# Four-layer gated cross-attention megakernel: an eight-headed layer's value products in 64-column tiles, row sums taken with the exponential, and a new order of steps

## What is computed

```python
x = x + tanh(g_xattn[0]) * diff_attention(LN(x), ctx)        # layer 0: 32 score heads of 8, values of 16
x = x + tanh(g_ffn[0])   * coupling_net(LN(x))
x = x + tanh(g_xattn[1]) * perceiver(ctx, LN(x), mask)       # layer 1: 8 heads of 64
x = x + tanh(g_ffn[1])   * moe_10_experts(LN(x))
x = x + tanh(g_xattn[2]) * attention(LN(x), ctx, ctx)        # layer 2: 16 heads of 16
x = x + tanh(g_ffn[2])   * attention_then_moe_8(LN(x))       # "f2": 16 heads of 8, then 8 experts
x = x + tanh(g_xattn[3]) * attention_one_head(LN(x), ctx, ctx)
x = x + tanh(g_ffn[3])   * quantised_mlp(LN(x))

# layer 1's attention, the one that the change edits
kv = concat([LN(ctx), LN(x)], axis=tokens) @ Wkv             # 512 keys
sim = (q * 64**-0.5) @ k.T * 64**-0.5                        # masked over the first 256 keys
out = softmax(sim) @ v                                       # 256 queries x 64, for each of 8 heads
out = layernorm(concat(heads) @ Wo)
```

## Time and profile before

| | |
|---|---|
| Time, median of 3 runs | 4502.43 us |
| Lowest, highest | 4487.78, 4503.43 us |
| Profiled execution | span 4493.2 us from first to last instruction; the profile gives no other time of this execution |
| TensorE | busy 4197.2 us (93%) |
| Weight loads | 3198.6 us (71%) |
| VectorE | 2949.1 us (66%) |
| ScalarE | 2085.8 us (46%) |
| GpSimd | 91.9 us (2%) |
| Chain that ended last | PE 80%, DVE 12%, ACT 5% |
| Granted TensorE clock, mean | 0.972 |

### The profile page before, as it was taken

One profiled execution on the slowest core, in us unless ns is written; L12 is line 12 of the kernel. 1 busy time (PEld: TensorE's weight loads), 2 busy tenths in 40 slices (PEclk: granted clock), 3 DMA queues, 4 the chain that ended last, 5 costly groups with the idle time before them and its releaser, 6 DMA issues.

```text
span 4493.2 us, 73928 instructions
## 1 busy us (share of the span) xinstructions
PE 4197.2 (93%) x28256; PEld 3198.6 (71%) x28256; DVE 2949.1 (66%) x7812; ACT 2085.8 (46%) x3424; POOL 91.9 (2%) x180
## 2 busy tenths in 40 slices
PE   7898998989989899898999999999999999999998
PEld 4675966759667596675966759667696676956768
DVE  6667776676656666666765767657676576665655
ACT  4544455353553435535355353553535535356342
POOL 0000000000000000000000000000000000000000
PEclk8999999999999999999999999999999999999999
DMA  2010610103001030010300103001030010300012
GB/s 99 1 45 10 217 37 1 52 23 132 29 15 41 24 128 29 15 41 29 123 29 15 41 29 123 29 15 41 29 123 29 15 41 29 123 29 15 31 55 102
DMA packets 51769, 228.06 MB, mean 51 GB/s; under 512 B 4832, under 2 KB 21216, under 8 KB 31584
## 3 DMA queue, kind: packets, MB, share of 16 engines
q1 hardware_dynamic: 51424, 223.33, 13.8%
HBM read 202.34 MB, written 20.97 MB: 50 GB/s over the span
## 4 chain that ended last, share of the span: by engine, by line
PE 80%; DVE 12%; ACT 5%; issue 3%; DMA 0%; SPq 0%; DVEq 0%; ACTq 0%
PE w L574 18%; PE w L584 12%; PE o L709 11%; PE w L830 8%; PE w L820 8%; PE w L642 4%; PE w L558 4%; PE o L702 3%; DVE mx L1243 3%; PE w L625 3%; PE w L677 2%; PE w L567 2%; PE w L721 1%; DVE nt L1184 1%; PE w L612 1%
## 5 line engine op out<-in xcount | busy, mean ns | idle before, releaser
L1243 DVE TENSOR_REDUCE mx<-w 128x4 f32<-128x1024 f32 x512 | 606.8, 1221 | 180.5 <-PE w L625 167.2
L975 ACT ACTIVATE pt_spread<-w 128x1024 f32<-128x1024 f32 x512 | 519.9, 1024 | 236.8 <-PE w L642 203.7
L709 PE MATMUL o<-pt_spread,va 128*32 128x256 f32 x4096 | 543.2, 396 | 30.5 <-ACT pt_spread L975 29.8
L921 ACT ACTIVATE oth<-w,res 128x256 f32<-128x256 f32 x656 | 276.9, 471 | 569.4 <-PE w L820 470.3
L574 PE MATMUL w<-xnT,stream 128*128 128x256 f32 x1792 | 413.1, 382 | 1.4 <-ACT xnT L913 0.8
L574 PEld LDWEIGHTS w<-xnT,stream 128*128 128x128 f32 x1792 | 338.2, 191 | 50.7 <-DVE x L1212 1.0
L709 PEld LDWEIGHTS o<-pt_spread,va 128*32 128x32 f32 x4096 | 205.0, 111 | 202.2 <-issue 63.3
L820 PE MATMUL w<-qodd,va_hi 128*128 128x256 f32 x2048 | 344.8, 283 | 1.1 <-issue 0.8
L820 PEld LDWEIGHTS w<-qodd,va_hi 128*128 128x128 f32 x2048 | 284.6, 188 | 7.8 <-issue 2.4
L1502 DVE TENSOR_REDUCE mx<-w 128x2 f32<-128x1024 f32 x128 | 155.8, 1225 | 199.2 <-PE w L679 198.9
L1212 DVE SCALAR_TENSOR_TENSOR x<-w,gate,x 128x256 f32<-128x256 f32 x512 | 223.2, 477 | 90.6 <-PE w L830 71.7
(11 more groups left out here) (263 smaller groups left out, 7722.5 us busy)
## 6 DMA issues: line engine op xcount, KB each, us to landing
stream_lo<-split SPq DMA_DIRECT2D x56, 1024.0 KB, 4.8
va_hi<-split SPq DMA_DIRECT2D x56, 1024.0 KB, 6.9
stream<-in_moe_dram SPq DMA_DIRECT2D x80, 384.0 KB, 3.1
stream<-in_resident_dram SPq DMA_DIRECT2D x8, 2048.0 KB, 7.4
raw<-in_moe_dram SPq DMA_DIRECT2D x8, 1024.0 KB, 6.8
split<-va_hi SPq DMA_DIRECT2D x8, 1024.0 KB, 8.9
split<-stream_lo SPq DMA_DIRECT2D x8, 1024.0 KB, 10.8
stream<-in_resident_dram SPq DMA_DIRECT2D x8, 1024.0 KB, 4.7
```

The source lines that it names most:

```text
L709: mm = pe.matmul(o[g:g + 32, 0:T], by_heads(plan, s)[:, kt, plan.v_of(h), :], p[:, a * 512 + kt * T:a * 512 + (kt + 1) * T], start=(kt == ...
L921: h = act.activation(dst[:, c, :], w[:, c * T:(c + 1) * T], func, bias=bias[:, c:c + 1], **more)
L975: act.activation(exp_buffer(plan.name + ".exp", s, u), w[:, :], ACT.Exp, scale=scale).then_inc(S["s_P"], 1)
L1243: dve.tensor_reduce(mx[s][:, :, 2 * v:2 * v + 2].rearrange("p t a -> p a t"), w[:, :].rearrange("p (a t k) -> p a t k", a=2, t=TT), AX_X, ...
```

## The change

The eight-headed layer's value products go two heads at a time into one bank: head `u` into partitions 0 to 63 or 64 to 127 by its parity, with 64 columns and a `tile_position`. The ones and their column of `va` are gone; the row sums are taken by the exponential's accumulated output. So an item is two heads, there are 4 evacuations and one `back` step of eight transposes of 128x128 for each element, and the scaling works on the layout of two heads. `ORDER` is laid out anew from end to end.

```diff
-        self.units_per_item = 4 // self.per_unit if group else 1
+        self.units_per_item = 2
...
 ORDER = (
-    "DAM11ADM11ADDAAMAAAA7AAAJAMAAAAAAAMA1AMMAMAD0M050M50M505M0M50M50M50M5M0550M50M50M5M0M505M0M55CC5HC0HCHCHCHCHC2H0CH0CHHC0"
+    "DAM11ADM11ADDAAMAAAA7AAAJAMAAAAAAAMA1AMAADM0M0M50M50M50M50M50M50M50M5M0550M50M50M50M550M0MM55CC5HCHCHCHCH0CHC0HHCC20H0HH"
...
-            va.append(sb(f"va{s}", [P, KT * L1_HEADS * (L1_DIM + 1)]))
-            va_hi.append(nc.alloc_sbuf_tensor_at(f"va_hi{s}", [P, MOE2_COLS], F32R, offset=nc.sbuf_base - KT * L1_HEADS * (L1_DIM + 1) * 4))
+            va.append(sb(f"va{s}", [P, KT * L1_HEADS * L1_DIM]))
+            va_hi.append(over(f"va_hi{s}", [P, MOE2_COLS]))
...
                 if plan is L1:
+                    g = L1_DIM * (u % 2)
                     for kt in range(KT):
-                        mm = pe.matmul(o[0:L1_DIM + 1, 0:T], by_heads1(s)[:, kt, u, :], p[:, kt * T:(kt + 1) * T],
-                                       start=(kt == 0), stop=(kt == KT - 1))
+                        mm = pe.matmul(o[g:g + L1_DIM, 0:T], by_heads1(s)[:, kt, u, :], p[:, kt * T:(kt + 1) * T],
+                                       start=(kt == 0), stop=(kt == KT - 1), tile_position=(0, g))
...
-                m = L1_DIM + 1 if plan is L1 else P
                 for i in range(4):
                     for tt in range(TT):
-                        mm = pe.transpose(w[:, i * T + tt * P:i * T + tt * P + m],
-                                          oth[s][0:m, i, tt * P:(tt + 1) * P], ident[0:m, 0:m])
+                        mm = pe.transpose(w[:, i * T + tt * P:i * T + (tt + 1) * P], oth[s][:, i, tt * P:(tt + 1) * P], ident)
...
-                evac(oth[s][0:m, i % 4, :], bank[0:m, 0:T], "s_oT")
+                evac(oth[s][:, i % 4, :], bank[:, 0:T], "s_oT")
...
                         h = act.activation(turned[s][u % 2][:, tt, :], w[:, tt * 512:(tt + 1) * 512], ACT.Exp,
-                                           bias=mx[s][:, tt, u:u + 1], scale=-1.0)
+                                           bias=mx[s][:, tt, u:u + 1], scale=-1.0,
+                                           accum_out=mx[s][:, tt, L1_HEADS + u:L1_HEADS + u + 1])
...
                 if plan is L1:
-                    v = w[:, :].rearrange("p (i t d) -> p i t d", i=4, t=TT)
-                    r = rc[:, 0:8].rearrange("p (i t) -> p i t", i=4)
-                    link(dve.reciprocal(r, v[:, :, :, L1_DIM]))
-                    o = ob[s][:, :].rearrange("p (t n i d) -> p t n i d", t=TT, n=2, i=4)
+                    dve.wait_ge(*after("s_soft", "l1.soft", s, L1.units - 1))
+                    r = rc[:, 0:TT * L1_HEADS].rearrange("p (t h) -> p t h", t=TT)
+                    link(dve.reciprocal(r, mx[s][:, :, L1_HEADS:2 * L1_HEADS]))
+                    v = w[:, :].rearrange("p (i t h d) -> p i t h d", i=4, t=TT, h=2)
+                    o = ob[s][:, :].rearrange("p (t i h d) -> p t i h d", t=TT, i=4, h=2)
+                    r = r.rearrange("p t (i h) -> p t i h", h=2)
                     for tt in range(TT):
-                        h = dve.tensor_tensor(o[:, tt, k], v[:, :, tt, 0:L1_DIM],
-                                              r[:, :, tt].unsqueeze(2).to_broadcast([P, 4, L1_DIM]), ALU.mult)
+                        h = dve.tensor_tensor(o[:, tt], v[:, :, tt], r[:, tt].unsqueeze(3).to_broadcast([P, 4, 2, L1_DIM]), ALU.mult)
...
                 if st == "l1":
-                    link(pool.memset(qodd[s][0:64, :, :].bitcast(F32), 0.0))
-                    ones = by_heads1(s)[:, :, :, L1_DIM:]
-                elif st == "l3":
+                    pool.memset(qodd[s][0:64, :, :].bitcast(F32), 0.0).then_inc(S["s_vinit"], 1)
+                    return
+                if st == "l3":
```

More of the change, by code:

```diff
@@ new lines @@
+    "HCCNCNCHHCNCC5CHC0NN0CHHC7C3C0HHH30C300C309009C089809C86968C6CCC8L6CK6LKCLKILCL0IIK0I99K8I089069C086L988C6C660LCKLJ0IKKI"
+    "I0L0CKLK0II0CFF0F00F000CC000C0C000C5050ACC50C50CC550C0CC557C5C0C0C0CHCHH00C0C0000HH00C00CH0C00HH0H0C00C000A55JCCC0CCCCC0"
+    "CC50CC50CC550CCC0C55C5C0CC0HCHCHC0HC0BHHCCH0HH0C7CCGC0C04JGBC9CC4L1860K9BI8C60LK9BCIL806K9DMICDB186L09KBCL8I09K6CL8I6B11"
+    "KA0AI9ACALAMA8BAK6I0C9L86DK0IDMC0A0JD0AA0C0AA0MC0M71AAC0CA0AAAAA0AAM0C0MC05050C50M50M50M5C0M50M5MMC5050MM50M50M50M50M5MM"
@@ new lines @@
+    "0CMMCCC55HHCC5H0CHCHCHCHCHCH0HHCC00HCHCHCH0C620HH60H6C020602C0CC000C0C0I0CI0ICI0C0ECE07020C0ECC0CCC0C0JC0CBC0E0BCB0C005B"
+    "0C0B50C050B505CB00CCCB0N0C550NCNC5HCCNCCH5CNHCH0CNCN0CCHHCNC0733CHH0H30C009C3009089C0896896F6C8CCCC6LL8CKKIJ6CLCLKKILK00"
+    "98I90II680968609C988CL660CLCK0KL0IKLII0CLKK0I0ICFF00F0C000000CC0C00A0C5050CC50C50CC550C0CCC555C70C0CCHCHCA000HH00000C00C"
+    "00HHC0C00HHJ0H0C00C00C055CC0C0CCCC55CC0CC05C0C5C0CCCC5545C740CC0HHCC00HC0HCHCHC01HHM0H1CGJC1C1CCA09CGCC8L6KIACLA09KAAI86"
@@ new lines @@
+    "AACL0K98AI6C0L9K8IAD6ACL09KI8A06C9L8AK6IAA09CL86AAKA0I9MD8C6D0710LAA0KAIJ00DD0CM00CMCMAC0MACC0C0CMM00C0M50M50M50M50M50M5"
+    "0M50M50M550M50M50M5M0MCMCM5500CCC55HHCC5HCHCH0C2HCHCHC0HHHC7C0HHCCH0CH0C60HH6E0H602C0602C0CC0E00C0C00ICI0ICI0C0C0200C0EC"
+    "C0CCC0C0C0JCBC0CB0CB005C0B00B5500E0CB055C0B0CCCB00NC550NCCN5HCCNCCH5CNCHH0CNN0CCCH7HN0CC33CHH3H30C00C00F9900C8980C968896"
+    "CCCC6LCKL6ILKCICLKL0KI08CK96II80990L8K89660CI69L88C660LKCCLKJ0ILK0IKII00C0F0F00CC000F000C00A0C05M0C5050C50C50CC5C0CC55CC"
@@ new lines @@
+    "5C0C0C7CMHCHC00HH000000C00C00HHC0C00HH0H0C00C000C55C0ACJC0CCCC55CC0C0C5C0C5C0CCC5C5745C40CC0HH0CC10H0CHCHCHC0HH0H1CGCC1J"
+    "1CCA0C9GCC8LAK60I9CADL86AAKAI09C8LA6AKAI0C9L86KD0I9C8L6AKIACL09KI86DAA09C8L6AAKI0D9AA86C0M0LAA0K7AI0010MCJM0CD0CMM0CCM00"
+    "AAC00C0M50M5M0505050CM50M50M50M5C5500CM55M0M0M50M50MMCMMCCC552HHCC57HCHCHC0HCHCHCH0HHCC02HHCCH0CH0C0HH660H0C60602C0C0C00"
+    "JC00C0ICI0ICI0EC0C0CE0C2C0C0CC0EC0C0C0CB0E0CBBC5000CB00B50050CB550CB00CCCB00N55C0NCNC5HCCNCNCHHCNCC5CHHC0NNC007CCHC3HHH3"
@@ L275 @@
+    "E0CJ002C0ECC0CCC0C0C0CBC0CB0CB5000ECC0B505CB00CCC0NCB550CB00NHC50BCN50HC0NCCN5HCCNCC5H0CN7N0CH0HCC3CHHH30C300C039F0908C8"
+    "09690C68968CCC6CLCLKCLKLICKI0C8IL6090KKL89C9IKI88I60L9068C6968L6CK0CK0LKLII0JKII000CFF0C00F000C000C0C000C5050C5C0C50CC55"
+    "0C0CC5C55C0C0CCHC0HC0H0H0C70000CH00C00H0C0HH0H0J0C00C0005C5C0CC0CCCC55CC0CC05C0C5C0CCC5C545C0CC00HCHCHCHCHCHC0HHH0CC0JCC"
+    "C00C79CC8LK0IC69L8K609ICL8K6ICL09K86IGCL09K8CI60LK98I09C68LK6I0C98L6K0IC400GC00C0C00CCCC00C0CC0C"
 )
```

64 lines of the change are left out of this document (22 added, 42 removed).

## The result

| | before | after |
|---|---|---|
| Time, median | 4497.83 us (4 runs, 4487.78 to 4503.43) | 4544.53 us (4 runs, 4540.51 to 4549.76) |
| After / before | | 1.0104, 95% interval 1.0086 to 1.0123 |
| Profiled execution: time, span | 4493.22, 4493.2 us | 4549.76, 4547.6 us |
| Granted TensorE clock, mean | 0.972 | 0.959 |

The change makes the kernel slower by 1.04%. The forecast was 4398 us, faster by 2.3%.

A forecast was written before the change was run, and what follows sets the result against it. TensorE was taken as the bound, busy 4197.2 of 4493.2 us. The eight-headed layer's 54 us (66 - 15 + 3) and the order's 50 sum to 104, taken from 4502.4 to give 4398 us; range 4335 to 4480.

The forecast's parts named there:

- A pair saves at most the 1.73 us of its second head, less the time by which that head's probabilities come late: Eight-headed layer's value products: 52 pairs of adjacent heads overlap in two column tiles, gaining 66 us after lateness.
- the last tile stands behind twelve others: Argument for 64-column overlap: 16 instructions of 32-column units in four tiles took only 1.03 us.
- The first rival: Eight-headed layer: 64-column tiles do not overlap, since the first head's instructions queue ahead; 4453 us, chance 0.08.
- Changes of tile shape: Eight-headed layer's value products: 76 runs entered and left, 152 changes at 0.10 us, 15 us lost.
- The accumulated output at 0.10: Eight-headed layer's exponentials on ScalarE: 256 row-sum outputs at 0.10 us each, bounds nothing and 0.20.
- So it costs nothing as long as TensorE has more to do than ScalarE: Eight-headed layer: row sums cost nothing, as two heads take TensorE 6.3 us and ScalarE at most 5.7.
- The 94 overlaps of 32 columns: New overlaps in layer 0, layer 2 and its expert layer's attention: 0.79 us each, 61 counted half, 50 us gained.
- Nothing else in the order do I put at a gain or a loss: Whole new order: apart from the overlaps and their changes of tile shape, its effect was put at zero.
- TensorE never stands: Layer 0's value products: TensorE has no idle time, so 33 new overlaps count in full, 26 us.
- signs of being wrong: 16 instructions in 3.4 us; L703's ScalarE waits over 30 us; layer 2 no shorter, more idle TensorE; exponentials much over 0.8 us.
- The one for slower: TensorE stands at the 167 paired runs, behind two score steps lacking a bank; at 1.0 us each 4565 us, chance 0.07.
- The freed time turns into waiting: TensorE waits for ScalarE and VectorE, swallowing two thirds or more; 10 to 35 us stay, about 4480, chance 0.09.

The follow-up runs named there:

- E3: Changed kernel with the products of two adjacent heads of different parity issued in turn: 4509.74 us, ratio 1.0047 to the kernel before.
- E4: Changed kernel without the exponential's accumulated output, row sums left out of the computation: 4528.11 us, ratio 1.0093 to the kernel before.
- E7: Kernel before, with the new order in layer 0's value products alone: 4481.78 us against 4501.41, ratio 0.9960.
- E1: Changed code with the old order, less its first `back` steps and one pair of steps exchanged: 4543.65 us against 4485.76, ratio 1.0120.
- E2: Code of the kernel before with the new order, a few steps of the eight-headed layer adapted: 4627.32 us, ratio 1.0313 to the kernel before.
- E5: Changed kernel with the old order in the experts' stretch alone: 4547.25 us, ratio 1.0115 to the kernel before.
- E9: E3 with the new order only in layer 0 and the eight-headed layer, old order from there to the experts' end: 4529.92 us, ratio 1.0095.
- E10: Kernel before, with the new order only from the eight-headed layer's last value products to the experts' end: 4574.88 us, ratio 1.0183.

## Why the prediction was wrong

**"A pair saves at most the 1.73 us of its second head, less the time by which that head's probabilities come late": wrong.** The second head costs 0.92 us (2.79 less 1.87) at the least, since its instructions can't pass the first head's. 52 pairs save at most 0.81 each, 42 us, where the forecast had 66. The lateness itself was no worse than thought: with the products in turn (E3), which start only when both heads are there, 46 of the 52 pairs take 1.88, and the waits ahead of them are 13.8 us, 0.27 a pair; 0.25 was taken for 41 of them and 1.2 for the other 11. The step that failed is the inference from "the last tile stands behind twelve others": those were four to a tile. The first rival named the danger ("have to be queued before the second head's first") and I argued it away. Its extreme, 0.22 us saved a pair, did not come either; by the Trainium skill's strict order of starts (TensorE: Matmul & The Clock Gate, Part 3, "The mechanism") no second head could start before the eighth instruction of the first, and the trace has it at the fifth.

**Changes of tile shape, 0.10 each: nearly right.** 0.09 at entry and at exit, and 0.05 more inside a run (its first step is 0.27, not 0.22): 0.24 for a single head against 0.20.

**The accumulated output at 0.10: half of what it is** (0.20). "So it costs nothing as long as TensorE has more to do than ScalarE" was close: 4 to 5 us by E4. But the comparison of 6.3 against 5.7 us per pair was one of sums, and a sum does not say when: in a pair's `exp`, `max`, `exp` the next softmax is due before ScalarE can have it.

**The 94 overlaps of 32 columns: right as work.** L710 lost 69.3 us with 123 us more at the low clock in the whole kernel; 50 were counted, 74 before halving. Layer 0 gave 20 of 26 us, in E7 18.

**"Nothing else in the order do I put at a gain or a loss": wrong, and this is what turned the sign.** Standing grew by 91.3 us: 27 in the eight-headed layer, 22 in the attentions, 14 in the experts, 13 in layer 0, where "TensorE never stands" was said of the order of before. The low clock, of which the sum has no term, grew by 123 us, at 0.35 some 43. The page had it beforehand: 0.93 in layer 2's stretch against 1.00 elsewhere. The account: +91 standing, +43 clock, and, as what remains, the rest of TensorE's work down by 80, where the forecast had 104: together +54. Of the signs of being wrong, layer 2's came: the attentions took 745.6 us against 746.8, with 22 us more standing.

**The rivals.** The one for slower was right in that standing ate the gain, but not on where: it put it at the pairs, behind two score steps for want of a bank. L710's and L703's own waits for ScalarE came to 25.5 us (29.8 at L709 before), and the wait for banks (L625 for VectorE) grew by 9.1. The rest stands at transposes, `exp` scores and other steps whose input is late, the transposes' wait by L1124 with 26.0 us more first of all. In size, the rival asked for 0.62 us of standing at each of 167 paired runs; there were 91 / 167 = 0.55, and with the clock 0.80. I gave it 0.07, on the ground that the kernel before meets few such waits, but a row of before speaks for the order of before. "The freed time turns into waiting" had a ceiling at no change that nothing in it justified: moving steps can make more waiting than the work that it saves. E1 and E2 show that code and order have to be priced together, since the same order costs 140 us with the old code.

What stays open: which steps of the new order cost the experts some 32 us, whether the changed use of the banks makes E1's later stretches longer, and why 11 of the 52 pairs start their second head at 1.18 us. No kernel tried here keeps the new order's overlaps in layer 2 without its standing, so that what they would be worth there is reckoned, not measured.

## What to carry to other kernels

When products into different column tiles are to run side by side, issue them in turn, or in blocks of at most four instructions (two fp32 products) a tile; eight in a row into one tile give away about half of the overlap. When a step is moved to sit beside its like, price the standing of all that now follow each other without it, and the low clock that comes with standing, not only the work that overlaps. And of a new order, take over the part by which its stretch gets shorter, where the two orders agree at its ends: layer 0's alone made this kernel faster than either, while the cuts of E5, E9 and E10 lost 27 to 36 us each on the way to the next pass, against the kernel before.

## What the runs showed of the hardware that was not expected

A column tile holds one running and three waiting instructions, and the next instruction for it blocks those for other tiles behind it (2.79, 2.33 and 1.90 us for blocks of 8, 6 and 4). Products into another tile start ahead of earlier ones in the program. An accumulated ScalarE output is a second instruction of 0.20 us. A us at the low clock costs 0.35 us in these stretches, and 0.41 over executions of one kernel, not the 0.5 of a halved speed; that waits cover the rest was not tested. Executions of one kernel differ by 20 us together with the granted clock (4483.6 us at 0.974, 4504.0 at 0.969). And eight needless transposes ahead of each of three waits an element raise the mean clock of the whole run from 0.959 to 0.977.
